# Transposing half of each expert's gathered rows on TensorE instead of all of them by DMA

## The chip, the cores and the metric

The kernel runs on one core of one Trainium2 chip, as one launch. The metric is the device time of one execution in microseconds (us); several executions are timed and the median is given. A core has five engines that run their own instruction streams and meet only at semaphores: TensorE (PE, with its weight loads PEld), VectorE (DVE), ScalarE (ACT), GpSimd (POOL) and SyncE (SP). Sixteen DMA engines move data for all of them. SP issues the ordinary and the transposing DMAs, on one queue; POOL issues the gathers, on another.

## The reference, cut to what matters

The program is one cross-attention layer with layernorm over 4096 tokens of width 512, and then a mixture of 16 experts. What the change touches is the expert part:

```
expert_inputs = dispatch(xn, gate_probs, cap=512)   # top 2 of 16 experts, 512 rows for each expert
gg = einsum('enc,ech->enh', expert_inputs, w_gate)  # 512 -> 256
h  = einsum('enc,ech->enh', expert_inputs, w_fc)    # 512 -> 256
h  = silu(gg) * h
o  = einsum('enh,ehc->enc', h, w_proj)              # 256 -> 512
y  = sum over the two choices of prob * o
x  = x + y
```

Everything is float32. The kernel keeps the precision by splitting each operand into two float16 numbers, high and low, and multiplying in three passes (high*high, high*low, low*high).

## The kernel before, in words

There are three stages, one after the other: `setup` (layernorm, queries, keys, values), `attend` (scores, softmax, output, the router's choice, and `rows_dram`, which holds for each token its normalised row as 512 high and 512 low halves, 2 KB in all), and `experts`.

`experts` handles the 16 experts one after the other, `e` = 0 to 15, with buffers that alternate by parity (`b`). For one expert:

- POOL gathers its 512 rows (`gather`, L1271): four indirect DMAs of 128 rows, one for each tile `j`, into `rows[:, b]` (128 partitions by 4 tiles by 1024 halves, 1 MB).
- The rows must be transposed, because TensorE contracts over partitions. SP issues one transposing DMA for the whole expert (`transpose_rows`, L1216 to L1218) from `rows[:, b]` to `xT[:, b]`, called `xTe` in the trace. For expert 0 it is four DMAs of one tile each (L1247). The gather for a buffer waits until the transpose that reads it has landed (L1277), and the gather of expert 1 waits for all four transposes of expert 0 (L1276).
- SP also loads the weights: `load_gf` (gate and fc weights, 1 MB, as soon as both raw buffers were converted), `load_p` (projection weights, 512 KB), `load_x1` (512 KB of the residual) and `store` (four tiles of 256 KB of output). All stand in SP's one order of `step` (L1220).
- ACT rounds the raw weights to the high half (`gf_high`, `p_high`), DVE computes the low half (`gf_low`, `p_low`).
- TensorE's `up` (L1448) computes four products of 12 matmuls into the PSUM banks `pg0` to `pg3`, 48 matmuls an expert. `down` (L1463) computes four output tiles of six matmuls into `po0` to `po3`, 24 an expert. The order in `step` (L1474) is up of expert e, then down of expert e-1.
- ACT takes tanh of a gate bank (`gate_tanh`), DVE forms the hidden activations (`hidden`), ACT copies each output tile out of its PSUM bank (`out_rows`). In ACT's `step` the order is weights of e+1, the two tanh of e, `p_high` of e, the four output tiles of e-1.

After the experts, POOL gathers two expert outputs for each token (`collect`, L1283), DVE adds them to the residual, and SP writes the result. POOL starts this only when all outputs of expert 15 have been stored (L1298).

The order on every engine is written out by hand; no planner moves anything.

Of the kernel before, what the change touches and what calls it, by code (L numbers as in the profile page):

```python
# [48 lines left out]
def build(nc, x, ctx_in, Wk, Wv, bv, Wq, bq, Wo, bo, w_router, w_fc, w_gate, w_proj, out):  # L49
# [29 lines left out]
    with ExitStack() as whole:  # L79
        def sem(name):  # L80
            return whole.enter_context(nc.semaphore(name))

        def sb(name, shape, dt, ctx=whole):
            return ctx.enter_context(nc.sbuf_tensor(name, shape, dt))

        ident = sb("ident", [P, P], F32)
        nhalf = sb("nhalf", [P, 1], F32)
# [1030 lines left out]
def experts(nc, v):  # L1118
    sb, sem = v["sb"], v["sem"]
    w_fc, w_gate, w_proj, out_t = (v[n] for n in ("w_fc", "w_gate", "w_proj", "out_t"))  # L1120
    x1_dram, rows_dram, eo_dram = (v[n] for n in ("x1_dram", "rows_dram", "eo_dram"))
    tbl_dram, TW, T, ident = v["tbl_dram"], v["TW"], v["T"], v["ident"]
    D, KT, NT, E, CAP, H = (v[n] for n in ("D", "KT", "NT", "E", "CAP", "H"))
# [5 lines left out]
    with ExitStack() as c_:  # L1129
# [34 lines left out]
        pg = [c_.enter_context(nc.psum_tensor(f"pg{i}", [P, 512], F32)) for i in range(4)]  # L1164
        po = [c_.enter_context(nc.psum_tensor(f"po{i}", [P, 512], F32)) for i in range(4)]

# [13 lines left out]
        wph, wpl = sem("wph"), sem("wpl")  # L1180
        x0_in = sem("x0_in")
        x_in = [sem(f"x_in{i}") for i in range(2)]
        u_pe = sem("u_pe")
# [8 lines left out]
        with nc.Block() as block:  # L1192
            @block.sync
            def _(sp):
# [21 lines left out]
                def transpose_rows(b):  # L1216

                    sp.dma_start_transpose(xT[:, b].rearrange("p j h k c -> p (j h k) c"), rows[:, b]).then_inc(x_in[b], 16)  # L1218

                def step(m, b, before, more_gf, more_p):  # L1220
                    e = 2 * m + b
                    if more_gf:

                        sp.wait_ge(wgl, 2 * (e + 2))
                        load_gf(e + 2)
                    elif more_p:

                        sp.wait_ge(u_pe, 4 * e)
                    if more_p:
                        sp.wait_ge(g_in[1 - b], 16 * J * (m + 1))  # L1230

                    if more_p and isinstance(m, int):
                        transpose_rows(1 - b)
                    load_x1(XT * e)
                    if more_p and not isinstance(m, int):
                        transpose_rows(1 - b)
                    if before:
# [6 lines left out]

                for j in range(J):
                    sp.wait_ge(g0_in[j], 16)
                    sp.dma_start_transpose(xT[:, 0, j].rearrange("p h k c -> p (h k) c"),  # L1247
                                           rows[:, 0, 2 * D * j:2 * D * (j + 1)]).then_inc(x0_in, 16)
                sp.wait_ge(wgl, 2)
# [17 lines left out]
            def _(pool):  # L1267
# [3 lines left out]
                def gather(e):  # L1271

                    if e == 1:
                        pool.wait_ge(x0_in, 16 * J)  # L1276
                    wait_for(pool, x_in[e % 2], 16 * ((e - 1) // 2))  # L1277
                    for j in range(J):
# [24 lines left out]
            def _(act):  # L1303
# [12 lines left out]
                def gate_tanh(e, h):  # L1316
                    act.wait_ge(u_pe, 4 * e + 2 * h + 1)
                    wait_for(act, h_rdy, 2 * e)
                    act.activation(th[:, h, :], pg[2 * h][:], ACT.Tanh, scale=0.5 / (XN_S * W_S)).then_inc(th_rdy, 1)

                def out_rows(e, j):
                    act.wait_ge(o_pe, J * e + j + 1)
                    wait_for(act, o_out[j], 16 * e)
                    act.activation(o_sb[:, j, :], po[j][:], ACT.Copy, scale=1.0 / (H_S * W_S)).then_inc(o_ev, 1)
# [3 lines left out]
                gf_high(0, 0)  # L1328

                def step(e, b, down, more):  # L1330
# [3 lines left out]
                    gate_tanh(e, 0)  # L1334
                    gate_tanh(e, 1)
                    p_high(e, b)
                    if down:
                        for j in range(J):
                            out_rows(e - 1, j)

# [12 lines left out]
            def _(dve):  # L1353
# [6 lines left out]
                def p_low(e, b):  # L1360
                    dve.wait_ge(wph, e + 1)
                    dve.scalar_tensor_tensor(out=wp[:, b, :, 1, :], in0=raw_p[:], scalar=W_S, in1=wp[:, b, :, 0, :],
                                             op0=ALU.mult, op1=ALU.subtract).then_inc(wpl, 1)

                def hidden(e, h, b):
# [45 lines left out]
                dve.drain()  # L1411
                dve.tensor_copy(cidx[:], crow[:]).then_inc(crow_rdy, 1)

                def step(e, b, more):
                    if more:
                        gf_low(e + 1, 1 - b)
                    hidden(e, 0, b)
                    hidden(e, 1, b)
                    p_low(e, b)

# [26 lines left out]
            def _(pe):  # L1447
                def up(m, b, u):  # L1448

                    e, h, w = 2 * m + b, u // 2, (wg, wf)[u % 2]  # L1450
                    if u == 0:
                        if isinstance(m, int) and m == 0 and b == 0:
                            pe.wait_ge(x0_in, 16 * J)
                        wait_for(pe, x_in[b], 16 * (m + b))
                        pe.wait_ge(wgl, 2 * (e + 1))
# [5 lines left out]
                    last.then_inc(u_pe, 1)  # L1461

                def down(e, j, b):  # L1463
                    if j == 0:
                        pe.wait_ge(h_rdy, 2 * (e + 1))
                        pe.wait_ge(wpl, e + 1)
                    wait_for(pe, o_ev, J * (e - 1) + j + 1)
                    for k in range(HT):
                        last = three_passes(pe, po[j][:],
                                            (hT[:, b, k, 0, j * P:(j + 1) * P], hT[:, b, k, 1, j * P:(j + 1) * P]),  # L1470
                                            (wp[:, b, k, 0, :], wp[:, b, k, 1, :]), k == 0, k == HT - 1)
                    last.then_inc(o_pe, 1)

                def step(m, b, before):  # L1474
                    for u in range(4):
                        up(m, b, u)
                    if before:
                        for j in range(J):
                            down(2 * m + b - 1, j, 1 - b)
# [6 lines left out]
                pe.wait_ge(grow_rdy, 1)  # L1486
                step(0, 0, False)
                step(0, 1, True)
                with pe.Fori(1, E // 2) as m:
                    for b in range(2):  # L1490
                        step(m, b, True)
                for j in range(J):
# [24 lines left out]
```

## Time and profile before

| | us |
|---|---|
| median of 3 executions | 1734.36 |
| lowest and highest | 1730.28 and 1741.48 |
| the profiled execution, device time | 1739.93 |
| its span in the trace | 1738.2 |
| TensorE busy | 1525.2 (88%) |
| VectorE busy | 799.6 (46%) |
| ScalarE busy | 397.7 (23%) |
| GpSimd busy | 354.9 (20%) |

The busy shares are averages over stages with different limits. In 40 slices of the span (43.5 us each) the page has, for TensorE's busy tenths, its granted clock, and the share of the DMA engines:

```profile
PE   7999989999999999999999999999962688989600
PEclk9999999999999999999999999999985899999855
DMA  6699733443353353354344345335336999999487
```

Setup is the first few digits, attention the long run of nines, the experts are slices 31 to 38, and the collecting of outputs is the last three. Only among the experts do TensorE and the DMA engines both stand near nine. In the rows further down a matmul's duration is longer than its pitch, since matmuls are pipelined: the distance between two starts is what one costs.

### The profile page before, as it was taken

To read this page: it belongs to the slowest core of one execution; us is meant where nothing else is said; L and a number is where in the kernel's file an instruction comes from. 1 tells how busy PE (TensorE), PEld (TensorE's weight loads), DVE (VectorE), ACT (ScalarE), POOL (GpSimd) and SP (SyncE) were. 2 spreads that over 40 slices of the span, in tenths; PEclk is the share of its full clock that TensorE was granted. 3 is DMA by queue.
4 is the path that set the end of the run, shared out by engine and by line. 5 is a ranking of instruction groups with operands and counts; after the bars stand their busy time and mean duration, and the time that the engine had idled before them with its cause. 6 is when DMAs were issued, how large, how long until landed. Compare 5 with 4: busy or idle time off the path is not lost. (4 is left out here: it accounts for less than half of the span.)

```text
span 1738.2 us, 23208 instructions
## 1 busy us (share of the span) xinstructions
PE 1525.2 (88%) x7449; PEld 697.7 (40%) x7449; DVE 799.6 (46%) x2196; ACT 397.7 (23%) x468; POOL 354.9 (20%) x477
## 2 busy tenths in 40 slices
PE   7999989999999999999999999999962688989600
PEld 3444444444444444444444444444421233434200
DVE  3566534445444444444544544444433344544254
ACT  2233312113113112112211311311201233333200
POOL 2244300111211111111111121111113212221275
PEclk9999999999999999999999999999985899999855
DMA  6699733443353353354344345335336999999487
GB/s 195 170 235 232 168 74 69 94 105 74 82 117 74 70 118 85 68 107 97 68 97 102 74 85 113 74 73 120 74 74 182 215 291 294 300 285 287 154 273 255
DMA packets 478541, 248.90 MB, mean 143 GB/s; under 512 B 377898, under 2 KB 427823, under 8 KB 478386
## 3 DMA queue, kind: packets, MB, share of 16 engines
q1 hardware_dynamic: 464768, 213.46, 51.4%
q0 software_dynamic: 12672, 35.10, 7.1%
q8 instruction: 12, 0.20, 0.0%
q10 hardware_dynamic: 1074, 0.02, 0.0%
q14 instruction: 15, 0.12, 0.0%
HBM read 104.11 MB, written 51.90 MB: 90 GB/s over the span
## 5 line engine op out<-in xcount | busy, mean ns | idle before, releaser
L44 PE MATMUL sc<-kT,qt 128*128 128x512 f16 (+1 forms) x896 | 315.5, 357 | 4.7 <-DMA qt<-q_dram 3.0
L45 PE MATMUL sc<-kT,qt 128*128 128x512 f16 (+1 forms) x896 | 315.1, 357 | 0.0
L46 PE MATMUL sc<-kT,qt 128*128 128x512 f16 (+1 forms) x896 | 313.4, 357 | 0.0
L46 PE MATMUL acc<-vv,pT 128*128 128x512 f16 x775 | 293.6, 379 | 0.0
L45 PE MATMUL acc<-vv,pT 128*128 128x512 f16 x775 | 293.6, 379 | 0.0
L44 PE MATMUL acc<-vv,pT 128*128 128x512 f16 x775 | 293.5, 379 | 0.0
L890 DVE TENSOR_SCALAR_CACHE_REDUCE s_sb<-sc 128x512 f32<-128x512 f32 (+1 forms) x224 | 141.1, 632 | 247.5 <-PE sc L46 247.4
L815 POOL TENSOR_TENSOR idf<-ia,ic 128x2 f32<-128x2 f32 x32 | 6.3, 197 | 759.5 <-DVE ia L992 759.5
L856 ACT ACTIVATE row<-xs 128x512 f16<-128x512 f32 x32 | 20.2, 632 | 589.0 <-DVE xs L939 589.0
L846 ACT ACTIVATE p_sb<-s_sb,negb 128x3202 f32<-128x3202 f32 x32 | 95.1, 2970 | 254.3 <-DVE negb L898 254.3
L44 PEld LDWEIGHTS sc<-kT,qt 128*128 128x128 f16 x896 | 87.7, 98 | 103.6 <-issue 12.9
L911 DVE TENSOR_TENSOR p_hl<-p_sb,p_hl 128x3200 f16<-128x3200 f32 x32 | 111.8, 3493 | 37.5 <-ACT p_hl L850 37.5
L46 PEld LDWEIGHTS sc<-kT,qt 128*128 128x128 f16 x896 | 87.8, 98 | 91.1 <-issue 0.8
L45 PEld LDWEIGHTS sc<-kT,qt 128*128 128x128 f16 x896 | 87.8, 98 | 87.7 <-issue 0.6
L46 PEld LDWEIGHTS acc<-vv,pT 128*128 128x128 f16 x775 | 75.7, 98 | 91.5
L1279 POOL DMA_INDIRECT rows<-rows_dram,gidx x64 | 69.3, 1083 | 204.5 <-DMA xTe<-rows 179.9
L45 PEld LDWEIGHTS acc<-vv,pT 128*128 128x128 f16 x775 | 75.7, 98 | 80.7
L44 PEld LDWEIGHTS acc<-vv,pT 128*128 128x128 f16 x775 | 75.6, 98 | 80.8
L44 PE MATMUL pg<-xTe,wg 128*128 128x512 f16 x128 | 52.5, 410 | 52.8 <-DMA xTe<-rows 52.8
L928 DVE SCALAR_TENSOR_TENSOR x<-acc,rinv,xb 128x512 f32<-128x512 f32 x32 | 24.0, 751 | 158.8 <-PE acc L1073 158.8
L850 ACT ACTIVATE p_hl<-p_sb 128x3200 f16<-128x3200 f32 x32 | 91.9, 2871 | 2.9
L1288 POOL DMA_INDIRECT got<-eo_dram,cidx x64 | 70.0, 1093 | 70.2 <-DMA eo_dram<-o_sb 51.0
(191 smaller groups left out, 2041.0 us busy)
## 6 DMA issues: line engine op xcount, KB each, us to landing
eo_dram<-o_sb SPq DMA_DIRECT2D x64, 256.0 KB
x_raw<-in_x_dram SPq DMA_DIRECT2D x32, 256.0 KB, 3.0
q_dram<-q_st SPq DMA_DIRECT2D x32, 256.0 KB, 2.7
qt<-q_dram SPq DMA_DIRECT2D x32, 256.0 KB, 2.8
x_in<-in_x_dram SPq DMA_DIRECT2D x32, 256.0 KB, 3.0
x_dram<-x SPq DMA_DIRECT2D x32, 256.0 KB, 3.0
rows_dram<-row SPq DMA_DIRECT2D x32, 256.0 KB, 2.2
raw_g<-in_L_ffn_w_gate_dram SPq DMA_DIRECT2D x16, 512.0 KB
```

Source lines behind the costliest of these rows:

```text
L44: pe.matmul(out, s_hi, m_hi, start=first, stop=False)
L45: pe.matmul(out, s_hi, m_lo, start=False, stop=False)
L46: return pe.matmul(out, s_lo, m_hi, start=False, stop=last)
L815: pool.tensor_tensor(idf[:], ia[:], ic[:], ALU.add)
L846: act.activation(p_sb[:], s_sb[:], ACT.Exp, bias=negb[:], scale=SM / (CTX_S * Q_S), accum_out=rsum[:]).then_inc(exp_done, 1)
L850: act.activation(p_hl[:, 0, :], p_sb[:, 0:NK * P], ACT.Copy).then_inc(p_hi, 1)
L856: act.activation(row16[:, 0:D], xs2[:], ACT.Copy, scale=XN_S).then_inc(xs_hi, 1)
L890: dve.tensor_scalar(s_sb[:, 512 * c:512 * c + width[c]], sc[c % 3][:, 0:width[c]], 1.0, None, ALU.mult, ALU.max, accum_out=mxc[:, c:c + 1] ...
L911: dve.tensor_tensor(p_hl[:, 1, :], p_sb[:, 0:NK * P], p_hl[:, 0, :], ALU.subtract).then_inc(p_lo, 1)
L928: dve.scalar_tensor_tensor(out=x1[:], in0=acc[:], scalar=rinv[:], in1=xb[:], op0=ALU.mult, op1=ALU.add).then_inc(x1_rdy, 1)
L1279: pool.indirect_dma_start(rows[:, e % 2, 2 * D * j:2 * D * (j + 1)], None, rows_dram, bass.IndirectOffsetOnAxis(ap=gidx[:, e, j:j + 1], ax ...
L1288: pool.indirect_dma_start(got[:, n % SETS, 2 * j + k, :], None, eo_dram, bass.IndirectOffsetOnAxis(ap=cidx[:, PER * n + j, k:k + 1], axis= ...
```

## The change

The gathered rows of an expert are four tiles. Tiles 2 and 3 are still transposed by DMA, in one DMA of half the size; tiles 0 and 1 are transposed on TensorE.

- TensorE: `rows_T` makes 8 transposes of 128x128 float16 for one tile, against an identity matrix `ident16`, into one PSUM bank (`tp0` or `tp1`, 1024 halves). In `step` the 16 transposes for expert e+1 stand between up of e and down of e-1. The last iteration is written out, so that it makes none.
- ACT copies `tp0` to `xT` (tile 0), after its two tanh and ahead of `p_high`. DVE copies `tp1` (tile 1), after `hidden` and ahead of `p_low`. ACT also makes `ident16` once.
- PSUM has eight banks. Two go to `tp`, so the output tiles have two banks in place of four: `down` of tile j now waits until tile j-2 was copied out.
- POOL's gather waits for TensorE's transposes of expert e-2 (`tp_pe`) and for their DMA half (`xt_dma`). The gather of expert 1 waits for nothing.
- SP: for expert 0 one DMA of two tiles, once tiles 2 and 3 have both been gathered, in place of four of one tile each. In `step` the loading of x1 and the transpose now stand ahead of `load_gf`, and wait for `u_pe` (up of e-1 done) in place of `wgl`.

```diff
-        po = [c_.enter_context(nc.psum_tensor(f"po{i}", [P, 512], F32)) for i in range(4)]
+        po = [c_.enter_context(nc.psum_tensor(f"po{i}", [P, 512], F32)) for i in range(2)]
+        tp = [c_.enter_context(nc.psum_tensor(f"tp{i}", [P, 2 * KT * P], F16)) for i in range(2)]
...
-                    sp.dma_start_transpose(xT[:, b].rearrange("p j h k c -> p (j h k) c"), rows[:, b]).then_inc(x_in[b], 16)
+                    sp.dma_start_transpose(xT[:, b, 2:4].rearrange("p j h k c -> p (j h k) c"),
+                                           rows[:, b, 2 * D * 2:2 * D * 4]).then_inc(xt_dma[b], 16)
...
+                    if more_p:
+                        wait_for(sp, u_pe, 4 * e)
+                        sp.wait_ge(g_in[1 - b], 16 * J * (m + 1))
+                    load_x1(XT * e)
+                    if more_p:
+                        transpose_rows(1 - b)
                     if more_gf:
-
                         sp.wait_ge(wgl, 2 * (e + 2))
                         load_gf(e + 2)
...
-                for j in range(J):
+                for j in range(2, 4):
                     sp.wait_ge(g0_in[j], 16)
-                    sp.dma_start_transpose(xT[:, 0, j].rearrange("p h k c -> p (h k) c"),
-                                           rows[:, 0, 2 * D * j:2 * D * (j + 1)]).then_inc(x0_in, 16)
+                transpose_rows(0)
...
-                    if e == 1:
-                        pool.wait_ge(x0_in, 16 * J)
-                    wait_for(pool, x_in[e % 2], 16 * ((e - 1) // 2))
+                    wait_for(pool, tp_pe, 2 * (e - 1))
+                    wait_for(pool, xt_dma[e % 2], 16 * (e // 2))
...
+                def rows_T(e, j, b):
+                    act.wait_ge(tp_pe, 2 * e + j + 1)
+                    act.activation(xT[:, b, j].rearrange("p h k c -> p (h k c)"), tp[j % 2][:],
+                                   ACT.Copy).then_inc(xt_act, 1)
...
+                    if more:
+                        rows_T(e + 1, 0, 1 - b)
                     p_high(e, b)
...
+                def rows_T(e, j, b):
+                    dve.wait_ge(tp_pe, 2 * e + j + 1)
+                    dve.tensor_copy(xT[:, b, j].rearrange("p h k c -> p (h k c)"), tp[j % 2][:]).then_inc(xt_dve, 1)
...
                     hidden(e, 1, b)
+                    if more:
+                        rows_T(e + 1, 1, 1 - b)
                     p_low(e, b)
...
-                        wait_for(pe, x_in[b], 16 * (m + b))
+                        pe.wait_ge(xt_act, e + 1)
+                        pe.wait_ge(xt_dve, e + 1)
+                        pe.wait_ge(xt_dma[b], 16 * (m + 1))
...
+                    for i in range(2 * KT):
+                        last = pe.transpose(tp[j % 2][:, i * P:(i + 1) * P],
+                                            rows[:, b, 2 * D * j + i * P:2 * D * j + (i + 1) * P], ident16[:])
+                    last.then_inc(tp_pe, 1)
...
-                    wait_for(pe, o_ev, J * (e - 1) + j + 1)
+                    wait_for(pe, o_ev, J * e + j - 1)
```

TensorE, one expert ahead of the loop (expert 1), with the semaphores that each instruction waits for. `pg` are the banks of up, `po` those of down, `tp` the new ones; `rows` is what was gathered. As changed, from the last matmul of up to the second wait in down:

```order
L46 MATMUL pg<-xTe,wf 128x512
L1487 MATMUL tp<-ident,rows 128x128 [waits xt_act,g_in0]
L1487 MATMUL tp<-ident,rows 128x128 x7
L1487 MATMUL tp<-ident,rows 128x128 [waits xt_dve]
L1487 MATMUL tp<-ident,rows 128x128 x7
L44 MATMUL po<-wp,hT 128x512 [waits wpl,h_rdy]
...
L44 MATMUL po<-wp,hT 128x512 [waits o_ev]
```

Before, down followed up directly; now 16 transposes stand between them, and the third output tile waits for `o_ev`.

SP in its loop, one half iteration. Before:

```order
L1196 ISA [waits wgl]
L1196 DMA raw_g<-in_L_ffn_w_gate_dram 128x4x256
L1197 DMA raw_f<-in_L_ffn_w_fc_dram 128x4x256
L1230 ISA
L1213 ISA [waits g_in1]
L1213 DMA x1s<-x_dram 128x2x512
L1218 DMA_TRANSPOSE xTe<-rows 128x32x128
```

And as changed:

```order
L1229 ISA [waits u_pe]
L1217 ISA [waits g_in1]
L1217 DMA x1s<-x_dram 128x2x512
L1222 DMA_TRANSPOSE xTe<-rows 128x16x128
L1234 ISA
L1200 ISA [waits wgl]
L1200 DMA raw_g<-in_L_ffn_w_gate_dram 128x4x256
L1201 DMA raw_f<-in_L_ffn_w_fc_dram 128x4x256
```

The transpose moved ahead of the megabyte of weights and of the wait for `wgl`, and has 16 blocks of 128 columns in place of 32. The four stores and the load of the projection weights follow in both.

## Rows read from the trace of the kernel before

**Rows 1.** Windows: us, busy time (x instructions) of each engine, PEclk, DMA share, GB/s

```profile
200.00:1306.00 1106.00, 1085.12 (x5559) 502.17 (x5557) 498.18 (x1699) 226.11 (x203) 143.45 (x233) 0.99 0.41 88
1306.00:1335.60 29.60, 0.67 (x3) 0.40 (x3) 7.47 (x29) 2.18 (x4) 7.10 (x10) 0.50 0.67 162
1335.60:1362.50 26.90, 12.88 (x48) 5.18 (x48) 10.77 (x13) 6.37 (x7) 8.37 (x8) 0.69 1.02 198
1362.50:1614.30 251.80, 227.03 (x1009) 99.48 (x1010) 116.64 (x152) 87.50 (x123) 56.68 (x52) 0.97 1.05 283
1614.30:1635.20 20.90, 20.84 (x97) 9.26 (x95) 6.21 (x10) 6.94 (x12) 0.00 (x0) 1.00 0.42 151
```

**Rows 2.** Who waited for whom, 1306 to 1738: total us, times, longest

```profile
POOL rows L1279 <- DMA xTe<-rows: 179.9, 14, 16.4
ACT o_sb L1324 <- PE po L46: 69.3, 64, 2.4
PE pg L44 <- DMA xTe<-rows: 52.8, 15, 14.1
```

**Rows 3.** Timeline of PE: start, us, instruction, idle before and its releaser

```profile
1335.63 0.58 PE L44 MATMUL pg<-xTe,wg 128*128 128x512 f16 x1 [14.09 <-DMA xTe<-rows]
1362.51 0.61 PE L44 MATMUL pg<-xTe,wg 128*128 128x512 f16 x1 [14.00 <-DMA xTe<-rows]
...
1366.76 0.63 PE L45 MATMUL pg<-xTe,wg 128*128 128x512 f16 x1
1367.18 0.63 PE L46 MATMUL pg<-xTe,wg 128*128 128x512 f16 x1
...
1401.48 0.38 PE L44 MATMUL pg<-xTe,wg 128*128 128x512 f16 x1 [3.55 <-DMA xTe<-rows]
...
1614.04 0.38 PE L46 MATMUL po<-wp,hT 128*128 128x512 f16 x1
1614.26 0.38 PE L44 MATMUL pg<-xTe,wg 128*128 128x512 f16 x1
```

**Rows 4.** Chain that ended last, in order of time, 1419 to 1448

```profile
1419.43 1.06 ACT wg L1307
...
1421.66 1.23 DVE wf L1357
...
1423.05 0.41 SPq L1196
...
1424.34 0.39 SPq L1213
...
1424.77 12.00 DMA xTe<-rows
...
1447.53 0.21 PE po L44
```

**Rows 5.** Timeline of SP's queue; the first is that of expert 1

```profile
1344.13 16.40 SPq L1218 DMA_TRANSPOSE xTe<-rows  x1
...
1451.95 2.17 SPq L1204 DMA_DIRECT2D eo_dram<-o_sb  x4
1454.22 0.41 SPq L1200 DMA_DIRECT2D raw_p<-in_L_ffn_w_proj_dram  x1
```

**Rows 6.** Windows in which transposes are most or all of the DMA traffic

```profile
1350.00:1355.00 5.00, 0.00 (x0) 0.00 (x0) 3.92 (x4) 1.06 (x1) 0.00 (x0) 0.57 1.21 90
...
1450.00:1452.00 2.00, 2.00 (x11) 0.93 (x10) 0.66 (x1) 1.15 (x2) 0.00 (x0) 1.00 1.28 290
```

**Rows 7.** Timeline of PE: the trace's own small matmuls

```profile
7.19 3.75 PE L555 MATMUL bank<-ident,w_b 128*128 128x128 f32 x16 [7.19 <-DMA w_b<-in_L_xattn_Wo_dram]
...
1189.15 0.25 PE L1080 MATMUL ps_m<-w_r,xrT 128*128 128x32 f16 x4
1189.25 0.24 PE L1083 MATMUL ps_m<-w_r,xrT 128*128 128x16 f16 x4
```

**Rows 8.** Timelines of ACT and DVE around the end of up at 1447.5

```profile
1445.47 1.05 ACT L1314 ACTIVATE wp<-raw_p 128x1024 f16<-128x1024 f32 x1
1448.94 0.60 ACT L1324 ACTIVATE o_sb<-po 128x512 f32<-128x512 f32 x1 [2.42 <-PE po L46]
...
1448.83 0.69 DVE L1378 TENSOR_TENSOR hT<-hf,hT 128x512 f16<-128x512 f32 x1
1449.44 1.22 DVE L1362 SCALAR_TENSOR_TENSOR wp<-raw_p,wp 128x1024 f16<-128x1024 f32 x1
```

**Rows 9.** Timeline of POOL: last gather of expert 0, first of expert 1

```profile
1327.78 1.00 POOL L1279 DMA_INDIRECT rows<-rows_dram,gidx  x1 [0.30 <-issue]
1336.32 1.00 POOL L1279 DMA_INDIRECT rows<-rows_dram,gidx  x1 [7.54 <-DMA xTe<-rows]
```

More of the change, by code:

```diff
@@ L86, in build @@
         ident = sb("ident", [P, P], F32)
+        ident16 = sb("ident16", [P, P], F16)
         nhalf = sb("nhalf", [P, 1], F32)
@@ L1121, in experts @@
     x1_dram, rows_dram, eo_dram = (v[n] for n in ("x1_dram", "rows_dram", "eo_dram"))
-    tbl_dram, TW, T, ident = v["tbl_dram"], v["TW"], v["T"], v["ident"]
+    tbl_dram, TW, T, ident, ident16 = v["tbl_dram"], v["TW"], v["T"], v["ident"], v["ident16"]
     D, KT, NT, E, CAP, H = (v[n] for n in ("D", "KT", "NT", "E", "CAP", "H"))
@@ L1180, in experts @@
         wph, wpl = sem("wph"), sem("wpl")
-        x0_in = sem("x0_in")
-        x_in = [sem(f"x_in{i}") for i in range(2)]
+        id_rdy = sem("id_rdy")
+        tp_pe = sem("tp_pe")
+        xt_act, xt_dve = sem("xt_act"), sem("xt_dve")
+        xt_dma = [sem(f"xt_dma{i}") for i in range(2)]
         u_pe = sem("u_pe")
@@ L1225, in step @@
                         load_gf(e + 2)
[L1226 to L1236, printed above, removed]
                     if before:
@@ L1323, in out_rows @@
                     wait_for(act, o_out[j], 16 * e)
-                    act.activation(o_sb[:, j, :], po[j][:], ACT.Copy, scale=1.0 / (H_S * W_S)).then_inc(o_ev, 1)
+                    act.activation(o_sb[:, j, :], po[j % 2][:], ACT.Copy, scale=1.0 / (H_S * W_S)).then_inc(o_ev, 1)
+                act.activation(ident16[:], ident[:], ACT.Copy).then_inc(id_rdy, 1)
                 act.wait_ge(d_rdy, 1)
@@ L1328, in _ @@
                 gf_high(0, 0)
+                rows_T(0, 0, 0)
                 def step(e, b, down, more):
@@ L1335, in step @@
                     gate_tanh(e, 1)
+                    if more:
+                        rows_T(e + 1, 0, 1 - b)
                     p_high(e, b)
                     if down:
-                        for j in range(J):
-                            out_rows(e - 1, j)
+                        out_rows(e - 1, 0)
+                        out_rows(e - 1, 1)
+                    if down:
+                        out_rows(e - 1, 2)
+                        out_rows(e - 1, 3)
                 step(0, 0, False, True)
@@ L1412, in _ @@
                 dve.tensor_copy(cidx[:], crow[:]).then_inc(crow_rdy, 1)
+                rows_T(0, 1, 0)
                 def step(e, b, more):
@@ L1451, in up @@
                     if u == 0:
-                        if isinstance(m, int) and m == 0 and b == 0:
-                            pe.wait_ge(x0_in, 16 * J)
-                        wait_for(pe, x_in[b], 16 * (m + b))
+                        pe.wait_ge(xt_act, e + 1)
+                        pe.wait_ge(xt_dve, e + 1)
+                        pe.wait_ge(xt_dma[b], 16 * (m + 1))
                         pe.wait_ge(wgl, 2 * (e + 1))
@@ L1461, in up, with rows_T @@
                     last.then_inc(u_pe, 1)
+                def rows_T(e, m, j, b):
+                    if isinstance(e, int) and e == 0:
+                        pe.wait_ge(g0_in[j], 16)
+                    elif j == 0:
+                        pe.wait_ge(g_in[b], 16 * J * (m + b))
+                    wait_for(pe, (xt_act, xt_dve)[j], e)
+                    for i in range(2 * KT):
+                        last = pe.transpose(tp[j % 2][:, i * P:(i + 1) * P],
+                                            rows[:, b, 2 * D * j + i * P:2 * D * j + (i + 1) * P], ident16[:])
+                    last.then_inc(tp_pe, 1)
                 def down(e, j, b):
@@ L1466, in down @@
                         pe.wait_ge(wpl, e + 1)
-                    wait_for(pe, o_ev, J * (e - 1) + j + 1)
+                    wait_for(pe, o_ev, J * e + j - 1)
                     for k in range(HT):
-                        last = three_passes(pe, po[j][:],
+                        last = three_passes(pe, po[j % 2][:],
                                             (hT[:, b, k, 0, j * P:(j + 1) * P], hT[:, b, k, 1, j * P:(j + 1) * P]),
@@ L1472, in down, with step @@
                     last.then_inc(o_pe, 1)
-                def step(m, b, before):
+                def step(m, b, before, more):
                     for u in range(4):
                         up(m, b, u)
-                    if before:
-                        for j in range(J):
+                    for j in range(2):
+                        if more:
+                            rows_T(2 * m + b + 1, m + b, j, 1 - b)
+                    for j in range(J):
+                        if before:
                             down(2 * m + b - 1, j, 1 - b)
@@ L1486, in _ @@
                 pe.wait_ge(grow_rdy, 1)
-                step(0, 0, False)
-                step(0, 1, True)
-                with pe.Fori(1, E // 2) as m:
+                pe.wait_ge(id_rdy, 1)
+                for j in range(2):
+                    rows_T(0, 0, j, 0)
+                step(0, 0, False, True)
+                step(0, 1, True, True)
+                with pe.Fori(1, E // 2 - 1) as m:
                     for b in range(2):
-                        step(m, b, True)
+                        step(m, b, True, True)
+                step(E // 2 - 1, 0, True, True)
+                step(E // 2 - 1, 1, True, False)
                 for j in range(J):
```

## The prediction

> **What bounds the kernel now.** I read the windows first, since the busy shares of the whole span mix three stages. The change acts between 1306 and 1635.2 us [rows 1]: attention ahead of it and the collecting of outputs behind it keep their instructions. Three stretches matter. From 1306 to 1335.6 TensorE has almost nothing to do: indices and rows of expert 0 are on their way. From 1335.6 to 1362.5 it works 12.88 of 26.9 us. From 1362.5 to 1614.3, that is from up of expert 1 to up of expert 15, 14 steps, it is busy 227 of 251.8 us at a granted clock of 0.97, while the DMA engines stand at 1.05. A step takes 251.8 / 14 = 17.99 us.
>
> What would it take if TensorE never waited? The last window answers that: up of expert 15 and two downs, 96 matmuls, in 20.9 us with the clock at 1.00 [rows 1], so 0.218 us each, and 72 of them 15.7 us. The loop is 14 * (17.99 - 15.7) = 32 us above that.
>
> The waits say whose that is: TensorE waited 52.8 us, 15 times, for the transposed rows and for little else [rows 2]. Two of the 15 are the starts of expert 0 and expert 1, 14.09 and 14.00 us; the other 13 are 24.7 us in all, such as the 3.55 us at 1401.48 [rows 3]. What is left of the 32 us, some 7, is the half clock after a longer wait: behind the wait of 14.00 us the pitch is 0.42 us, against 0.22 later [rows 3]. That is the lower of the two clocks, 1.2 instead of 2.4 GHz. The same engine that waits is thus also made slow by waiting.
>
> Why are the rows late? The chain of waits has a loop [rows 4]: ACT converts the gate weights once it is through with the last output tile (1419.43), DVE finishes the low half of the fc weights (1421.66, 1.23 us), only then SP issues the next weights (1423.05) and x1 (1424.34), and the transpose behind these lands 12.00 us after its issue at 1424.77. So it stands behind 1.5 MB on its own queue, and beside the gather. Its price as pure traffic is small: between 1450 and 1452 transposes alone run at 290 GB/s [rows 6], 3.6 us for 1 MB. But from 1350 to 1355, with a gather still under way, the engines are as busy (1.21) and move 90 GB/s; SP is held for 16.40 us by the one issue of expert 1 [rows 5].
>
> **The change, part by part.** The sum is made against the profiled execution, 1739.93 us, which is 5.6 above the median of 1734.36.
>
> *The order on SP.* The transpose no longer waits for the converted weights nor stands behind the new ones. Let T be the end of up of expert e-1. SP is free for the transpose of e+1 after the last store and the projection weights, which before came 6.7 us after the end of up (1454.22 against the first matmul of down at 1447.53) [rows 4, 5]; the 16 new transposes put about 1 us on top, so T + 8. It is wanted at the start of up of e+1, two steps of about 16.6 us later less up itself (10.4), so T + 23. Half a transpose has 15 us for what a whole one did in 12.00 [rows 4]. Behind it the weights of e+2 leave at about T + 12 and are wanted at T + 24. Both have room, so all 13 waits and the half clock behind them can go: -32.
>
> *16 transposes a step on TensorE.* No row shows a float16 transpose of 128x128. The nearest below: a matmul's pitch goes with its columns, 0.218 us for 512, so 0.054 for 128; and that a weight load for every small matmul does not bind is seen at 1189.15, where four float16 matmuls with their own weights take 0.10 us to the start of the next four [rows 7]. The nearest above is the trace's own 16 float32 transposes, 3.75 us, 0.234 each [rows 7]. I take 0.06, near the float16 rows, since type and weight load are the same there, and the float32 row shares only the operation. Experts 2 to 15: 14 * 16 * 0.06 = +13 us (12 to 52). The step is then 15.7 + 1.0 = 16.6 us.
>
> *The copies.* ACT's copy of 1024 columns is like `p_high`, 1.05 us, DVE's like `p_low`, 1.22 [rows 8]. In the loop both end before down does (5.2 us): DVE's hidden values are ready 2.0 us after up (1449.52 against 1447.5) [rows 8], the copy at 3.3. Cost 0; without down as a cover, as between expert 0 and 1, it is 3.3 us of waiting.
>
> *Two banks for the output tiles.* Down of tile 2 waits until tile 0 was copied out. ACT does the copy of xT (T + 0.5 to 1.6), `p_high` (to 2.6), tile 0 (to 3.2). TensorE is through tile 1 at 1.0 + 2.6 = 3.6. Later tiles: a copy of 0.60 against 1.3 us of matmuls. Today it is ACT that waits for TensorE's tiles, 69.3 us in 64 waits [rows 2]. Cost 0, with 0.4 us in hand; each microsecond by which ACT is later than that costs 14.
>
> *Expert 1.* Its gather waits for nothing now. It was issued at 1336.32, after the last gather of expert 0 at 1327.78 [rows 9], and can follow 1.3 us behind it. So its transpose is issued at about 1340 in place of 1344.13, and it has half the size. Up of expert 1 started 14.0 us after up of expert 0 was through; the floor is the 3.3 us of DVE's copy. I take 5, as transpose and gather may meet in the slow way of 1350: -9 us (-10.7 to 0).
>
> *Expert 0.* Its DMA part cannot start before tiles 2 and 3 are both there, and then it meets the gather of expert 1. Before, four small transposes were spread over the gathers. I take +3 us (0 to +8: the same 0.5 MB at 90 GB/s takes 6).
>
> Sum: -32 + 13 - 9 + 3 = -25 us, so 1715 for the profiled execution and 1709 against the median. Everything behind 1635.2 moves forward unchanged.
>
> **The rivals.**
>
> *The DMA engines stay the bound.* The loop moves 283 GB/s * 17.99 us = 5.1 MB a step [rows 1]; without 0.52 MB it is 4.6 MB, and at the same rate 16.2 us, only 0.4 under TensorE's 16.6. For it: the share of 1.05, and that transposes and gathers together fall to 90 GB/s. Against it: part of the low rate comes from the order, not the load, and at 290 GB/s half a transpose less frees 1.8 us a step. If the step becomes 17.3, the loop gives 10 us, and with 6 at the start it is 1718.
>
> *ACT's column is late.* If the projection weights land after T + 1.6, or the copy out of PSUM is slower than 1.05, the second pair of output tiles waits in each step. ACT had 0.4 us to spare in my count. One microsecond a step gives -11, so 1723. Against it: raw_p leaves SP a whole step before it is wanted.
>
> *Transposes cost their own latency, and the kernel becomes slower.* If the 16 do not stream, but each costs the 0.234 us of the float32 ones, TensorE's step is 15.7 + 3.7 = 19.4 us and takes over as the bound: 14 * (19.4 - 17.99) = +20, with -9 + 3 and some 3 more for expert 1 it is +17, so 1751. The change decides at 0.17 us for a transpose, (32 + 6) / 224. Against it: the float16 rows stream. The Trainium skill speaks for it (TensorE: Matmul & The Clock Gate, section PE-mode transpose): it gives about 275 ns for a transpose in a kernel's context, since the access to SBUF dominates; by that figure, an estimate, it would be 4.4 us a step and about 1761 us. Whether that latency hides behind the next transpose no row here shows.
>
> *The change does nothing there.* If the 13 waits were for something else that ends just after the transpose, they would stay. ACT and DVE are busy 87.50 and 116.64 of the 251.8 us [rows 1], and the new order takes the weights off the transpose's path; I give this little.
>
> **How the numbers follow.** The forecast 0.62, at 1709, its own range 1700 to 1717 (price of a transpose 0.054 to 0.08, start -11 to 0, and 3 us for the spread of the medians); DMA bound 0.20, at 1718; ACT's column 0.08, at 1723; slow transposes 0.07, at 1751; nothing gained 0.03, at 1734. The range 1700 to 1727 takes in the first three and leaves about 0.07 below and 0.13 above. One per cent, about what can be told from no change here, is 17 us, so the border is at 1717: faster is the forecast and a third of the DMA case, 0.68; slower is most of the slow transposes, 0.06; the same 0.26.
>
> **What would show it.** TensorE's waits for xTe from expert 2 on gone or below 5 us in all, the clock at 1.00 there. Starts of up 16.6 us apart, with 16 transposes at a pitch of 0.06. DMA share of the loop below 1.0 at about 280 GB/s. Up of expert 1 some 5 us after up of expert 0. Third tile of down without a wait for o_sb. It is wrong if the starts of up are 17 us or more apart: with waits for xTe it is the DMA case, with waits for o_sb ACT's column, with no waits the price of the transposes.

## The result, and the profile after

The kernel with the change takes 1709.36 us (median of 4 executions, 1705.76 to 1714.88). The kernel before, run beside it, took 1736.74 (median of 4, 1730.28 to 1741.48). The ratio is 0.985, 95% interval 0.980 to 0.989: faster, by about 27 us. The profiled execution took 1711.6 us with a span of 1709.9, against 1738.2 before.

The windows of the change, cut at its own starts of up of experts 0, 1 and 15, answer to those of [rows 1]. The columns are busy time of PE, PEld, DVE, ACT and POOL, each with its count, then granted clock, DMA share and GB/s.

```profile
1305.80:1339.00 33.20, 2.72 (x19) 1.96 (x20) 7.61 (x25) 3.46 (x5) 11.10 (x14) 0.50 0.69 169
1339.00:1353.60 14.60, 12.80 (x64) 5.91 (x65) 8.04 (x12) 5.33 (x7) 5.73 (x5) 0.90 1.12 248
1353.60:1585.90 232.30, 230.60 (x1233) 110.92 (x1234) 127.61 (x169) 102.82 (x139) 55.64 (x52) 1.00 1.02 275
1585.90:1606.80 20.90, 20.84 (x97) 9.27 (x95) 6.21 (x10) 6.93 (x12) 0.00 (x0) 1.00 0.43 151
```

In the third window, the loop of 14 steps, TensorE is busy 230.6 of 232.3 us at full clock: it is now the bound there. Yet the DMA engines are nearly as full as before, 1.02 at 275 GB/s against 1.05 at 283 [rows 1].

The waits of the whole program (engine, what waited, for what: us in all, how many, the longest), which answer to [rows 2]:

```profile
POOL rows L1276 <- DMA xTe<-rows: 141.1, 13, 13.2
ACT o_sb L1326 <- PE po L46: 34.9, 50, 2.3
PE pg L44 <- DMA xTe<-rows: 12.0, 4, 10.4
PE pg L44 <- DVE xTe L1376: 1.8, 1, 1.8
```

TensorE's waits for `xTe` fell from 52.8 us to 12.0. Where the rest is shows in TensorE's timeline (start, duration, instruction, wait before it), the starts of up of experts 0 to 3 (before: [rows 3]):

```profile
1339.02 0.59 PE L44 MATMUL pg<-xTe,wg 128*128 128x512 f16 x1 [10.37 <-DMA xTe<-rows]
1353.62 0.38 PE L44 MATMUL pg<-xTe,wg 128*128 128x512 f16 x1 [1.81 <-DVE xTe L1376]
1370.73 0.39 PE L44 MATMUL pg<-xTe,wg 128*128 128x512 f16 x1 [0.52 <-DMA xTe<-rows]
1388.02 0.38 PE L44 MATMUL pg<-xTe,wg 128*128 128x512 f16 x1 [0.68 <-DMA xTe<-rows]
```

10.37 us of the 12.0 stand ahead of expert 0. In the loop only three short waits are left, 1.7 us in all. From expert 3 on the steps are 16.43 us, except one of 17.07.

The span became 28.3 us shorter. Stage by stage, from the starts of up and of the first gather:

| stretch | before | after | difference |
|---|---|---|---|
| to the first gather of expert 0 | 1323.59 | 1322.59 | -1.0 |
| first gather to up of expert 0 | 12.04 | 16.43 | +4.4 |
| up of expert 0 to up of expert 1 | 26.88 | 14.60 | -12.3 |
| 14 steps, to up of expert 15 | 251.8 | 232.3 | -19.5 |
| to the end of the last down | 20.9 | 20.9 | 0 |
| collecting the outputs | 103.1 | 103.2 | +0.1 |

The 1.0 us ahead of the experts is a difference between two executions; the change touches nothing there.

### The profile page after: what moved, and what is told of

The parts are those of the page before. It is cut to its first block and busy times, and to the rows that moved or that the text cites. A ratio compares the mean times of both kernels' runs of the same rounds, so it can differ in the third digit from the quotient of the medians.

```text
span 1709.9 us, 23814 instructions
## 1 busy us (share of the span) xinstructions
PE 1526.6 (89%) x7705; PEld 710.1 (42%) x7705; DVE 807.4 (47%) x2212; ACT 412.9 (24%) x485; POOL 356.0 (21%) x477
## 5 line engine op out<-in xcount | busy, mean ns | idle before, releaser
L891 DVE TENSOR_SCALAR_CACHE_REDUCE s_sb<-sc 128x512 f32<-128x512 f32 (+1 forms) x224 | 141.1, 632 | 246.7 <-PE sc L46 246.7
L1276 POOL DMA_INDIRECT rows<-rows_dram,gidx x64 | 69.6, 1088 | 173.0 <-DMA xTe<-rows 141.1
L1455 DVE SCALAR_TENSOR_TENSOR x1s<-got,cw,x1s 128x512 f32 x64 | 45.3, 749 | 59.7 <-DMA got<-eo_dram,cidx 58.5
```

What stands on the lines that cost most here:

```text
L891: dve.tensor_scalar(s_sb[:, 512 * c:512 * c + width[c]], sc[c % 3][:, 0:width[c]], 1.0, None, ALU.mult, ALU.max, accum_out=mxc[:, c:c + 1] ...
L1276: pool.indirect_dma_start(rows[:, e % 2, 2 * D * j:2 * D * (j + 1)], None, rows_dram, bass.IndirectOffsetOnAxis(ap=gidx[:, e, j:j + 1], ax ...
L1455: last = dve.scalar_tensor_tensor(out=y, in0=got[:, i, 2 * j + q, :], scalar=cw[:, i, 2 * j + q:2 * j + q + 1], in1=y, op0=ALU.mult, op1=A ...
```

## The experiments

Experiments of one group ran on one chip and share their runs of the kernel before: 1735.69 us for 1, 2, 3 and 5; 1735.52 for 4, 6, 7 and 8; 1736.21 for 9 to 12. Ratios are to the kernel before, with 95% intervals. Where nothing else is said, an edit is one to the changed kernel. Long lines of the edits are cut with `...`, and waits and counts of semaphores that only follow an edit are left out.

**1. Only the new order on SP,** all four tiles by DMA (edit to the kernel before):

```
+ wait_for(sp, u_pe, 4 * e); sp.wait_ge(g_in[1 - b], ...)
+ load_x1(XT * e)
+ transpose_rows(1 - b)
  sp.wait_ge(wgl, 2 * (e + 2)); load_gf(e + 2)     # was ahead of these
```

> The kernel before with one edit: in SP's step the loading of x1 and the transpose (all four tiles, by DMA) stand ahead of the next gate and fc weights and wait for up of e-1, as in the change. TensorE transposes nothing. Theory A (order and half the load are both needed): a whole transpose issued some 7 us after the end of up of e-1 has 14 us until it is wanted, and meets the gather; the loop stays at 17 to 18 us a step, time 1722 to 1737. Theory B (the order alone was the brake): waits for xTe from expert 2 on fall to near 0, a step is 15.6 us, and the time is about 1737 - 33 = 1704, below the changed kernel.

Measured: 1734.91 us, 0.999 (0.997 to 1.001). Its window of the loop, and its waits:

```profile
1361.80:1618.00 256.20, 231.10 (x1008) 100.74 (x1009) 118.76 (x154) 91.14 (x125) 61.62 (x52) 0.95 1.07 280
PE pg L44 <- DMA xTe<-rows: 52.6, 13, 14.0
POOL rows L1273 <- DMA xTe<-rows: 178.1, 14, 15.1
```

Nothing moved: 52.6 us of waits as before, the DMA engines at 1.07. Part of my argument against the DMA rival was that the low rate comes from the order. That falls. A whole transpose, ahead of the weights, is as late as behind them.

**2. The changed kernel with the old order,** weights first:

```
+ if more_gf: sp.wait_ge(wgl, 2 * (e + 2)); load_gf(e + 2)
  wait_for(sp, u_pe, 4 * e); ...; load_x1(XT * e); transpose_rows(1 - b)
- if more_gf: sp.wait_ge(wgl, 2 * (e + 2)); load_gf(e + 2)
```

> The changed kernel with SP's old order: the next gate and fc weights, and the wait for wgl, stand ahead of x1 and the transpose again. Theory A: half a transpose behind 1.5 MB lands 1 to 2 us sooner than a whole one did and TensorE's own transposes cover another 1 us, so some waits come back: 1 us a step at most, 1712 to 1722. Theory B (the order alone): the gain in the loop (20 us) is gone, about 1730. Theory C (the smaller load alone): no waits, as the changed kernel, 1707 to 1711.

Measured: 1717.30 us, 0.989 (0.986 to 0.992). So the smaller share for DMA, with what comes with it, brings some 18 of the 27 us alone. In the profile the loop takes 236.8 us in place of 232.3: of its 14 steps three take about 18.2 us, two about 17, the others 16.4 to 16.7. The waits for `xTe` in that stretch are 4 in number and 4.1 us in all, the longest 1.61 us. The first of the long steps, that of expert 1, holds none of them; it starts at half clock, after a wait of 3.3 us. After the wait of 1.61 us the clock stays full. The first row is the window behind the wait of 3.3 us, the second the one behind that of 1.61:

```profile
1355.37:1359.37 4.00, 4.00 (x11) 1.51 (x12) 1.81 (x2) 0.15 (x1) 3.07 (x2) 0.57 0.63 153
1474.68:1478.68 4.00, 4.00 (x19) 1.88 (x20) 2.85 (x3) 1.52 (x2) 2.81 (x3) 1.00 0.99 325
```

The order takes most of this away: by the medians it is worth some 8 us once the load is lighter, and nothing (experiment 1) without that. The intervals of the two ratios overlap slightly.

**3 and 12. The kernel before, with the gather of expert 1 free** (two profiles of the same kernel; the median is that of the executions beside the first):

```
- if e == 1: pool.wait_ge(x0_in, 16 * J)
+ if e == 2: pool.wait_ge(x0_in, 16 * J)
```

> The kernel before with one edit: the gather of expert 1 no longer waits for the four transposes of expert 0 (the gather of expert 2 does). If the early gather is what shortened the gap before expert 1 in the change, the gap of 14.0 us falls by 6 to 9 us, expert 0 starts up to 3 us later: time 1728 to 1733. If the gap was made by the slow whole transpose meeting a gather, and only its half size helped, the gap stays above 10 us and the time is 1735 to 1738.

> A second profile of the kernel before with the gather of expert 1 let free. Its first profile shows the gap before expert 1 fallen by 10 us, its start at 1354.84 in place of 1362.51, and the end of TensorE's work 7.2 us earlier, while the medians of the timed runs differ by 1 us only. If the gain is kept, the loop from expert 1 to 15 takes 250 to 253 us here too; if it is given back in most executions, 256 us or more.

Measured: 1734.60 us, 1.000 (0.998 to 1.001). The starts of up of experts 0 and 1, in the first and the second profile:

```profile
1338.57 0.58 PE L44 MATMUL pg<-xTe,wg 128*128 128x512 f16 x1 [18.08 <-DMA xTe<-rows]
1354.84 0.39 PE L44 MATMUL pg<-xTe,wg 128*128 128x512 f16 x1 [4.06 <-DMA xTe<-rows]
```

```profile
1343.00 0.58 PE L44 MATMUL pg<-xTe,wg 128*128 128x512 f16 x1 [21.75 <-DMA xTe<-rows]
1359.72 0.39 PE L44 MATMUL pg<-xTe,wg 128*128 128x512 f16 x1 [4.07 <-DMA xTe<-rows]
```

The wait of expert 1 falls from 14.0 to 4.1 us. But expert 0 starts 16.0 and 19.7 us after its first gather, against 12.0 before, since its four transposes now run beside that gather. The loop takes 252.2 and 252.6 us, 251.8 before, so nothing is given back there. The profiles' spans, 1730.9 and 1735.7 against 1738.2, allow 2 to 7 us of gain; the medians show 1, less than the 3 to 8 I had expected. An early gather alone is mostly a swap between expert 1 and expert 0. Up of expert 1 starts 38.9 us after the first gather before, 32.3 and 36.4 here, and 31.0 in the change, where only half is left to transpose by DMA; what the half does to this without the early gather was not tried.

**4. Each transpose on TensorE made twice:**

```
- for i in range(2 * KT):
+ for i in [*range(2 * KT)] * 2:
```

> The changed kernel with each of TensorE's transposes made twice into the same place: 16 more transposes for every expert. If they stream at 0.056 us and TensorE is the bound, each of the 14 steps grows by 0.89 us, 16.43 to 17.3, and the time by 12.5 us plus about 1 at expert 1, less the 1.7 us of waits: 1720 to 1723. If the loop had slack on TensorE, it grows by less than 5 us.

Measured: 1724.88 us, 0.994 (0.992 to 0.997), 15.5 above the change and 2 above the upper end of what I expected. From expert 4 on the steps are 17.32 to 17.33, so 0.89 to 0.90 us for 16 transposes more: 0.056 each. The whole loop is 244.8 us against 232.3, 12.5 more, as expected; the rest of the 15.5 is not in it. That is the same as the pitch within the change (below).

**5. DMA transposes for experts 0 and 1 alone:**

```
- if more_p:
+ if more_p and isinstance(m, int) and e == 0:
      transpose_rows(1 - b)
```

> The changed kernel without the DMA transposes of experts 2 to 15: it leaves out the transposing of their tiles 2 and 3, and TensorE multiplies what experts 0 and 1 left there. If TensorE is the bound of the loop, the starts of up stay 16.43 us apart, only the waits of experts 2, 3 and 6 (1.7 us) go, and the time is 1706 to 1709. If the DMA engines still bound the loop, each step loses the 1.8 us of half a transpose or more and the time falls to 1690 or below.

Measured: 1711.05 us, 0.986 (0.983 to 0.989), no different from the change, and 2 us above the upper end of the first range. The second, 1690 or below, is far off.

```profile
1356.96:1587.03 230.07, 230.07 (x1233) 111.15 (x1234) 127.02 (x169) 101.92 (x139) 59.79 (x52) 1.00 0.75 244
```

Without the loop's DMA transposes TensorE is busy 230.07 of 230.07 us. A quarter of the DMA engines' time is free and nobody profits from it: the change left 2.2 us in the loop for a lighter DMA side, no more. They do not show in the time, since in this profile expert 0 starts 18.3 us after its first gather (16.4 in the change) and its step is 15.6 us (14.6), though the edit touches nothing there. So much do two executions differ at the start. The window also shows what half a transpose costs the DMA engines, (1.02 * 232.3 - 0.75 * 230.07) / 14 = 4.6 us a step for 0.5 MB; [rows 6] gives 1.8 us at a share of 1.28, that is 2.3.

**6. One tile on TensorE, three by DMA:**

```
- sp.dma_start_transpose(xT[:, b, 2:4]..., rows[:, b, 2 * D * 2:2 * D * 4])
+ sp.dma_start_transpose(xT[:, b, 1:4]..., rows[:, b, 2 * D:2 * D * 4])
- for j in range(2):
+ for j in range(1):
      if more: rows_T(2 * m + b + 1, m + b, j, 1 - b)
```

> The changed kernel with one tile for TensorE (copied by ACT) and three by one DMA. TensorE's step would be 15.54 + 0.45 = 16.0 us. If the DMA side has room, the time falls by 14 * 0.45 = 6 us, to 1703. If half a transpose was already just in time (in the changed kernel it landed 0 to 3 us ahead of its use), three quarters come too late, waits for xTe return, 0.5 to 1.5 us a step, and the time is 1709 to 1722. I expect the second.

Measured: 1720.90 us, 0.991 (0.989 to 0.994). The steps scatter from 16.11 to 19.41 us.

```profile
PE pg L44 <- DMA xTe<-rows: 9.7, 6, 3.4
PEld po L44 <- ACT o_sb L1326: 9.9, 14, 1.9
1544.45 1.06 ACT L1311 ACTIVATE wp<-raw_p 128x1024 f16<-128x1024 f32 x1 [0.98 <-DMA raw_p<-in_L_ffn_w_proj_dram]
```

Both waits that I had feared for the change itself are here: rows that come too late, and an output tile that ACT has not copied out. For this the weight loads waited 14 times, and the matmuls stood still in three cases, 3.5 us in all. In the row shown ACT is late because the projection weights of `p_high` were late.

**7. All four tiles on TensorE,** no DMA transpose, ACT and DVE copy two tiles each, and down of tiles 0 and 1 stands between the two pairs of transposes:

```
+ for h in (0, 2):
+     for j in (h, h + 1): rows_T(2 * m + b + 1, m + b, j, 1 - b)
+     for j in (h, h + 1): down(2 * m + b - 1, j, 1 - b)
```

> The changed kernel with all four tiles transposed on TensorE and no DMA transpose at all; tiles 2 and 3 stand between the second and third output tile, ACT copies tiles 0 and 2, DVE 1 and 3. TensorE's step is 15.54 + 1.78 = 17.3 us, 12.5 us more in the loop; expert 0 starts up to 6 us sooner, since it waits for no DMA transpose, and the 1.7 us of waits go. Together 1712 to 1717. If the DMA engines were the bound, it would be faster than the changed kernel.

Measured: 1721.36 us, 0.993 (0.990 to 0.995); 4 us above the upper end of what I expected. The loop went as expected: steps of 17.32 us with TensorE busy all the time and the DMA engines at 0.71.

```profile
1370.10:1595.20 225.10, 225.10 (x1353) 114.78 (x1352) 125.96 (x169) 107.34 (x143) 53.86 (x47) 1.00 0.71 233
```

But expert 0 starts only 3.7 us sooner after its first gather, not 6, its step takes 16.29 us (14.60 in the change), and the step of expert 1 takes 19.01 us since it begins at half clock. Just ahead of it stand transposes between waits of 0.67, 0.47 and 1.16 us. By tiles on TensorE, with the new order: 0, 1, 2 and 4 tiles give 1734.9, 1720.9, 1709.4 and 1721.4 us. Two is the best of these; three was not tried. The kernel with none lacks the free gather of expert 1.

**8. Expert 0 wholly on TensorE:**

```
- for j in range(2, 4): sp.wait_ge(g0_in[j], 16)
- transpose_rows(0)
+ rows_T(0, 2, 0)                 # ACT, behind rows_T(0, 0, 0)
+ rows_T(0, 3, 0)                 # DVE, behind rows_T(0, 1, 0)
- for j in range(2):              # PE
+ for j in range(J):
      rows_T(0, 0, j, 0)
```

> The changed kernel, but all four tiles of expert 0 are transposed on TensorE, which is idle there; from expert 1 on as in the change. In the changed kernel expert 0's DMA half took 8.30 us from its issue at 1330.47 to its landing, since it met the gather of expert 1. Without it expert 0 is ready some 2 to 3 us after its last gather at 1330.5: up of expert 0 starts at 1333 in place of 1339, all later work moves with it if the weights of expert 1 keep up: 1703 to 1706. If expert 1's transpose then is late, the gain at expert 0 is lost before expert 1: 1708 to 1710.

Measured: 1709.86 us, 0.985 (0.981 to 0.989): like the change. Expert 0 starts 4.2 us sooner after its first gather (12.2 against 16.4), but the following steps are 15.46, 18.89 and 18.12, with this at expert 2, and by expert 3 all but 0.7 us of the lead is gone:

```profile
1370.09 0.39 PE L44 MATMUL pg<-xTe,wg 128*128 128x512 f16 x1 [2.29 <-DMA xTe<-rows]
```

The transpose of expert 2, 16.7 us from issue to landing, sets the pace there, and what follows the wait costs as much again: the granted clock falls to half,

```profile
1371.09:1373.09 2.00, 2.00 (x6) 0.65 (x5) 0.64 (x1) 1.34 (x2) 1.61 (x2) 0.50 1.07 384
```

and the step is 18.12 us in place of 16.43, without a wait for expert 3's rows. TensorE can't be early when the DMA side has no slack.

**9. The residual's loads two steps later,** so that none stands ahead of the first two transposes of the loop:

```
- load_x1(XT * e)
+ if not isinstance(m, int) or m > 0: load_x1(XT * (e - 2))
  ...
+ load_x1(XT * (E - 2)); load_x1(XT * (E - 1))   # behind the last step
```

> The changed kernel with each load of x1 (512 KB, needed only after the experts) issued two steps later, the last two after step 15. If the DMA engines hold back experts 1 to 3, less traffic there lets the waits of experts 2 and 3 (1.2 us) go and the time falls by 1 to 2 us, to 1707 to 1709. If those waits only come from the slow meeting of transpose and gather, nothing changes, 1709 to 1710.

Measured: 1711.21 us, 0.986 (0.984 to 0.988), above both ranges. All steps of the loop are now 16.43 us and TensorE ends 2.7 us sooner. But the two loads at the end stand ahead of the last stores; the first collecting gather comes 6.7 us after TensorE's end, where in the change it was 3.5, so it starts at the same time:

```profile
1610.71 1.00 POOL L1288 DMA_INDIRECT got<-eo_dram,cidx  x1 [56.55 <-DMA eo_dram<-o_sb]
```

```profile
1610.28 1.00 POOL L1285 DMA_INDIRECT got<-eo_dram,cidx  x1 [54.67 <-DMA eo_dram<-o_sb]
```

The first row is this experiment's, the second the change's.

**10. Edits 8 and 9 together:**

> Both edits: expert 0's tiles all on TensorE, and x1 two steps late. With expert 0 alone the 4.2 us won at its start were lost again by expert 3. If DMA traffic in that stretch took them back, the lighter traffic keeps 2 to 5 us of them: 1704 to 1707. If something else did, 1708 to 1710.

Measured: 1707.60 us, 0.984 (0.981 to 0.986). Expert 0 starts early, the first step is 15.34 and all others are 16.43: what experiment 8 lost at expert 2, the later loads give back. The median is 2.3 us below that of experiment 8, and lies just above the range for this case.

**11. And matmuls without use while expert 0's rows arrive:**

```
+ for _ in range((1, 8, 1, 0)[j]): pe.matmul(po[0][:], ident16[:], rows[:, 0, 0:D], ...)
+ for _ in range(12): pe.matmul(po[0][:, 0:P], ident16[:], ident16[:], ...)
```

> As the run with both edits, and TensorE fills its waits for the gathers of expert 0 with matmuls whose results nobody uses (10 of 512 columns, 12 of 128), so that up of expert 0 starts at full clock. Its first 11 matmuls took 0.43 us in place of 0.22 each: 2.3 us less, if the rest follows, 1702 to 1705; no gain if expert 1 or 2 waits for its rows anyway.

Measured: 1705.24 us (1704.12 to 1706.83), 0.982 (0.980 to 0.984), the fastest kernel of the study. Its first matmul of up:

```profile
1335.51 0.38 PE L44 MATMUL pg<-xTe,wg 128*128 128x512 f16 x1 [0.16 <-issue]
```

It is a matmul of 0.38 us, where the change has 0.59 in the same place, and the first step falls from 15.34 to 13.22 us: that was half clock alone. Against the change the intervals overlap. Beside experiment 10 on the same chip (1706.78 to 1707.81) four of the five executions lie lower, at 1704.12 to 1705.35, and the fifth, at 1706.83, within its range.

## Why the prediction was right, and where it was not

The forecast was 1709 and 1709 came. That it agrees to one microsecond is luck: the sum said -25 us, the two profiles differ by 28.3 and the medians by 27.4, and the forecast started from the 1734.36 us of three executions, where the kernel before had 1736.74 beside the change. Term by term:

**The loop: predicted -32 + 13 = -19, measured -19.5.** What remains above 14 steps of 16.43 us is 232.3 - 230.0 = 2.3 us, the three waits and what follows them. The step without transposes, 16.43 - 0.89 = 15.54, is the 15.7 of the last window [rows 1]; the last step before, from 1598.71 to 1614.26, took 15.55.

**The transposes: predicted 0.06 us each, measured 0.056.** In the chain of the change they are one piece:

```profile
1364.14 0.89 PE tp L1487 x16
```

14 * 0.89 = 12.5 us. The rival with 0.234 each, and with it the Trainium skill's 275 ns (TensorE: Matmul & The Clock Gate, section PE-mode transpose), does not come true. The trace agrees with a duration of that order, 0.219 us for each transpose, but the next one starts 0.056 us later, so it is hidden behind the following ones; that section gives a duration and no pitch. Experiment 4 shows it a second time. Choosing the row by type and weight load, not by the operation's name, was right.

**Expert 1: predicted -9, measured -12.3.** Up of expert 1 starts 2.9 us after the end of up of expert 0 (1350.76 to 1353.62), not 5, so the gap fell by 11.1 us, just outside my range. The other 1.1 us are up of expert 0 itself, 11.74 us in place of 12.88, with fewer matmuls at half clock, which I had not counted. In the gap it is the copy of DVE that ends last, as I had it, but this takes 0.68 us and not the 1.22 of `p_low` [rows 8]:

```profile
L1320 ACT ACTIVATE xTe<-tp 128x1024 f16<-128x1024 f16 x16 | 16.4, 1024 | 39.8 <-PE tp L1487 39.8
L1376 DVE COPY xTe<-tp 128x1024 f16<-128x1024 f16 x16 | 10.9, 684 | 0.2 <-PE tp L1487 0.2
```

**Expert 0: predicted +3, measured +4.4.** As foreseen, its DMA part, issued at 1330.47, met the gather of expert 1 and took 8.30 us for 0.5 MB. Experiment 8 gives the 4.2 us back, and loses them later.

**ACT's column: predicted 0, measured 0.** TensorE never waited for `o_sb`. Experiment 6 shows that this rival was real: it came true in a neighbour of this kernel.

**The step that does not hold** is "Half a transpose has 15 us for what a whole one did in 12.00", with "Both have room" behind it. The 12.00 us of [rows 4] are one of the short ones. From issue to landing the 14 whole transposes of experts 2 to 15 took 7.9 to 19.2 us before, the median 13.9; the halves in the change take 8.8 to 15.0, the median 11.2. Half the bytes take a fifth less time, not half of it. For experts 2, 3 and 6 there was no room, those are the three short waits; the other halves land 0.7 to 5.1 us ahead of their use. Expert 3 is the worst: its half is issued at T + 8.7 (T the end of up of expert 1, 1363.98) and needs 15.03 us:

```profile
1371.36 1.00 POOL L1276 DMA_INDIRECT rows<-rows_dram,gidx  x1 [13.22 <-DMA xTe<-rows]
1372.65 15.03 DMA xTe<-rows
```

The first row, of the timeline, is the gather of expert 4; the second, of the chain, the transpose of expert 3, issued 1.3 us behind it. POOL issues each gather when the last reader of its buffer has landed (141.1 us of waits above, still 13 of them), and the next transpose is issued soon behind: 1.3 to 3.6 us for experts 2 to 9, 5.2 to 6.5 us for experts 10 to 14. In the first case the two meet. What that does shows in the DMA queues of the change. The columns are packets, MB and share of the 16 engines' time; q0 carries POOL's gathers, q1 the transposes and all else of SP. From 1435 to 1436, in the transpose of expert 6:

```profile
q1 hardware_dynamic: 228, 0.06, 125.5%
q0 software_dynamic: 9, 0.03, 7.4%
```

and from 1468 to 1469, in that of expert 8, with no packet of a gather left:

```profile
q1 hardware_dynamic: 1135, 0.29, 127.7%
```

While a few packets of the gather are still under way, q1 moves 0.06 MB in a microsecond, 60 GB/s, with the engines full. Without them it is 0.29 MB, 290 GB/s, as in [rows 6]. The slow meeting lasts 4 us and more for experts 2, 3, 5, 6 and 7 and 2 to 3 us for 4 and 8; these halves land after 11.9 to 15.0 us. From expert 9 on the gather is over, but for traces, when the transpose's packets move, and they land after 8.8 to 10.5 us. The loop cut in two, up to expert 8 and behind it, shows the same:

```profile
1353.60:1470.00 116.40, 114.70 (x613) 55.00 (x614) 64.51 (x85) 51.03 (x69) 30.68 (x28) 1.00 1.08 270
1470.00:1585.90 115.90, 115.90 (x622) 55.93 (x621) 63.09 (x84) 51.79 (x71) 24.96 (x24) 1.00 0.96 279
```

In the second part my figures hold, a share below 1.0 at about 280 GB/s; in the first they do not. I had seen the slow pair [rows 6] and still priced the transpose in the loop at its rate alone. Before the change it was rare: behind expert 1 only the transpose of expert 2 ran beside a gather for long (19.2 us to its landing), the others moved at 0.29 MB in a microsecond once the weights and x1 ahead of them were through. With the weights first, in experiment 2, it is again expert 2 alone, and the halves have a median of 10.3 us. So the new order, which issues the transpose sooner, also brings it closer to the gather.

The DMA rival (0.20, step 17.3) was thus half right: the DMA side is close to the bound. It does not set the step because TensorE's 16.43 us are just longer. Experiment 1 (no slack, no gain) and experiment 5 (all the slack, 2.2 us in the loop) stand on either side. In experiment 9 the residual's load no longer stands ahead of the transpose: the halves land after 8.0 to 11.2 us, the slow meeting is left at expert 2 alone, and the short waits are gone. The term of the sum came out right because it asked only whether the transpose is in time, and it is, by little. The DMA case should have had a higher chance.

**What the gain is made of.** No part does it alone: the order 0.999, the free gather 1.000, the lighter DMA load with the free gather 0.989, all together 0.985.

**Open:** which resource gather and transpose share, and which of the two holds up the other; the rows show only that they are slow together. No kernel was written to keep the two apart in time; from expert 9 on the change does so by itself, and there TensorE is the bound either way.

## What to carry to other kernels

When a transfer is late, ask first whether its engines are full: here reordering a queue whose engines were at 1.05 moved nothing, taking load off them did, and only then was the order worth something. Move work to the other engine until the two sides are about equal (here two tiles of four was the best tried; one and four both lose 12 us), and give to each side its slack in microseconds, not as "room". Take that slack from all transfers of a kind and not from one row: the one in [rows 4] was shorter than most. A start gained early, when the resource behind it has no slack, was given back within a few steps here.

## What the runs showed of the hardware that I had not expected

- A transposing DMA beside the tail of a gather moves 60 GB/s with the engines full, without it 290; a gather's share of 7% goes with it. In the loop 0.5 MB of transposes cost 4.6 us of the 16 engines' time, where the rate of the transposes alone [rows 6] would make it 2.3.
- DVE copies 128x1024 float16 from PSUM to float16 in 0.684 us; its pass over 128x1024 float32 with a second input, `p_low`, took 1.22 [rows 8]. ACT takes 1.02 for the same copy.
- 16 transposes of 128x128 in float16 take 0.89 us within a stream of matmuls, and the granted clock stays at 1.00 through the loop.
- Waits of 1.61 us in experiment 2 and of 1.81 us ahead of expert 1 in the change were followed by full clock, 1.00 in the 4 us behind them; the wait of 2.29 us in experiment 8 and that of 3.3 us in experiment 2 were followed by a granted clock of 0.50. In experiment 7 waits of only 0.67, 0.47 and 1.16 us with transposes between them were, too. 22 matmuls without use ahead of expert 0 took 2.1 us off its step.
